# First softplus of a fused four-layer kernel: mask and polynomial moved from VectorE to GpSimd, the first drive and decay begun per half

## What is computed

```python
x = silu(conv(in_proj(ctx)) + conv_b)                 # u, 256 channels x 1024 tokens
dt_low, B, C = split(x_proj(x))
dt = softplus(dt_proj(dt_low) + dt_b)                 # delta
A = -exp(A_log)
for each token:                                       # for each of 16 states
    state = state * exp(dt * A) + (dt * u) * B        # decay, drive
    y = sum(state * C)
```

## Time and profile before

| | |
|---|---|
| Time of 3 runs, median (lowest to highest) | 925.41 us (924.95 to 927.92) |
| The profiled execution: time, span | 922.5 us, 920.6 us |
| Granted TensorE clock, mean | 0.927 |
| Busy: TensorE (matmul) | 831.2 us, 90% |
| Busy: VectorE | 646.9 us, 70% |
| Busy: ScalarE | 437.7 us, 48% |
| Busy: GpSimd | 439.3 us, 48% |
| Chain that ended last | TensorE 66%, VectorE 16%, GpSimd 6%, ScalarE 3% |

### The profile page before, as it was taken

One profiled execution on the slowest core, in us unless ns is written; L12 is line 12 of the kernel. 1 busy time (PEld: TensorE's weight loads), 2 busy tenths in 40 slices (PEclk: granted clock), 3 DMA queues, 4 the chain that ended last, 5 costly groups with the idle time before them and its releaser, 6 DMA issues.

```text
span 920.6 us, 12557 instructions
## 1 busy us (share of the span) xinstructions
PE 831.2 (90%) x4270; PEld 529.2 (57%) x4270; DVE 646.9 (70%) x1008; ACT 437.7 (48%) x825; POOL 439.3 (48%) x305
## 2 busy tenths in 40 slices
PE   7987888979999999998998979999996989989992
PEld 3322333336888888875776445555565865646661
DVE  4888999988999999987465556778758384322222
ACT  5752335332777777762555616655545412123330
POOL 3016666782588888862498002525501431613331
PEclk9986889797999999999999959999998997999996
DMA  6431222712122222212001113332135010261114
GB/s 234 168 141 69 71 76 81 326 58 96 47 92 93 92 92 92 92 46 69 18 1 35 56 37 87 97 108 74 53 104 197 1 69 0 87 201 47 47 46 159
DMA packets 28917, 81.86 MB, mean 89 GB/s; under 512 B 3424, under 2 KB 17648, under 8 KB 27472
## 3 DMA queue, kind: packets, MB, share of 16 engines
q1 hardware_dynamic: 26464, 73.38, 23.2%
q0 software_dynamic: 2256, 6.18, 1.9%
q10 hardware_dynamic: 144, 1.57, 0.4%
HBM read 65.77 MB, written 17.35 MB: 90 GB/s over the span
## 4 chain that ended last, share of the span: by engine, by line
PE 66%; DVE 16%; issue 6%; POOL 6%; ACT 3%; DMA 2%; SPq 0%; DVEq 0%; POOLq 0%; ACTq 0%
PE ps L853 12%; PE ps L875 6%; PE ps L1818 5%; PE ps L1442 5%; PE ps L565 4%; PE ps L1822 4%; PE ps L1860 3%; PE ps L995 3%; PE ps L556 3%; PE ps L1339 3%; POOL ZT L1078 2%; PE ps L1461 2%; PE ps L323 2%; PE ps L865 2%; DVE stats L300 2%
## 5 line engine op out<-in xcount | busy, mean ns | idle before, releaser
L853 PE MATMUL ps<-W,ZT 128*128 128x256 f32 x512 | 120.9, 379 | 0.0
L646 POOL TENSOR_TENSOR M<-M 128x1024 f32<-128x1024 f32 x32 | 75.3, 2354 | 85.8 <-DVE M L481 47.4
L1889 ACT ACTIVATE N<-ps 128x512 f32<-128x512 f32 x128 | 69.5, 595 | 77.8 <-PE ps L1822 77.8
L731 POOL TENSOR_TENSOR M<-N,M 128x1024 f32<-128x1024 f32 x32 | 76.3, 2385 | 52.8 <-DMA M<-dbl_scratch 27.2
L853 PEld LDWEIGHTS ps<-W,ZT 128*128 128x128 f32 x512 | 92.4, 190 | 10.0
L1818 PE MATMUL ps<-M,W 32*128 32x256 f32 x512 | 76.9, 434 | 10.9 <-DVE W L1916 5.7
L1910 DVE TENSOR_REDUCE W<-ps 128x4 f32<-128x1024 f32 x64 | 78.1, 1221 | 11.6 <-PE ps L1822 8.3
L701 DVE TENSOR_TENSOR_SCAN ps<-ps,M 128x512 f32<-128x512 f32 x64 | 78.7, 1230 | 6.1
L1822 PE MATMUL ps<-W,M 32*128 32x256 f32 x512 | 82.0, 415 | 0.0
L565 PE MATMUL ps<-M,ident 128*128 128x512 f32 x128 | 74.8, 738 | 7.4 <-DVE M L671 7.4
L662 DVE TENSOR_TENSOR_SCAN M<-ps,M 128x1024 f32<-128x1024 f32 x32 | 73.3, 2290 | 7.6 <-ACT ps L612 3.0
(11 more groups left out here) (305 smaller groups left out, 1738.2 us busy)
## 6 DMA issues: line engine op xcount, KB each, us to landing
M<-dbl_scratch SPq DMA_DIRECT2D x48, 512.0 KB, 3.7
W<-in_gu SPq DMA_DIRECT2D x1, 4800.0 KB, 18.0
W<-in_gu SPq DMA_DIRECT2D x1, 4352.0 KB, 14.1
slot_scratch<-in_slots SPq DMA_DIRECT2D x1, 3999.0 KB, 16.7
att_scratch<-W SPq DMA_DIRECT2D x28, 128.0 KB
M<-slot_scratch SPq DMA_DIRECT2D x3, 1032.0 KB, 9.7
W<-in_gu SPq DMA_DIRECT2D x2, 1536.0 KB, 7.6
W<-in_dn SPq DMA_DIRECT2D x1, 2176.0 KB, 18.9
```

Source lines behind the costliest of these rows:

```text
L646: nc.gpsimd.tensor_tensor(dBu[:, t, :], du[0][:, t, :], Bb[:, par, :], ALU.mult).then_inc(S("dBu_rdy"), 1)
L731: nc.gpsimd.tensor_tensor(dBu[:, t, :], du[1][:, t, :], Bb[:, par, :], ALU.mult).then_inc(S("dBu1_rdy"), 1)
L853: last = nc.tensor.matmul(ps[:, UBANK[j % 2], e * DIM:(e + 1) * DIM], ZT[:, c, t * P:(t + 1) * P], gu[:, c, 2 * j + e, :], start=(c == 0), ...
```

## The change

Mask and polynomial of the first softplus go from VectorE to GpSimd, as four instructions per half (the fused step of VectorE is two there). VectorE waits for them per half (`sp_poly`), and does A's sign and the clear of the PSUM columns between the halves. GpSimd's first drive waits for half 0 of `du` alone, but stands behind `softplus0_gpsimd` in GpSimd's stream. ScalarE begins the first decay of each half when that half's `du` is done, and evicts the second layer's step sizes behind each of the two decays instead of ahead of both; the store of the ternary weights is issued behind them.

```diff
-        def steps_to_sbuf(act, l, bank):
-            for t in range(2):
+        def steps_to_sbuf(act, l, bank, halves=(0, 1)):
+            for t in halves:
...
-        def softplus0_vector(dve, link):
-
-            small = lambda t: dA[:, t, :].bitcast(mybir.dt.uint32)
+        def softplus0_gpsimd(pool, link):
+
             for t in range(2):
                 e, q = dBu[:, t, :], hC[:, t, :]
-                dve.wait_ge(S("sp_exp"), 2 * t + 3)
-                link(nc.vector.tensor_scalar(dA[:, t, :], e, 2.0 ** -7, None, ALU.is_lt))
-                dve.wait_ge(S("sp_exp"), 2 * t + 4)
-                link(nc.vector.tensor_tensor(q, q, e, ALU.mult))
-                link(nc.vector.scalar_tensor_tensor(q, q, 1.0, e, ALU.add, ALU.mult))
+                pool.wait_ge(S("sp_exp"), 2 * t + 3)
+                link(nc.gpsimd.tensor_scalar(dA[:, t, :], e, 2.0 ** -7, None, ALU.is_lt))
+                pool.wait_ge(S("sp_exp"), 2 * t + 4)
+                link(nc.gpsimd.tensor_tensor(q, q, e, ALU.mult))
+                link(nc.gpsimd.tensor_scalar(q, q, 1.0, None, ALU.add))
+                nc.gpsimd.tensor_tensor(q, q, e, ALU.mult).then_inc(S("sp_poly"), 1)
+
+        def softplus0_vector(dve, link):
+
+            small = lambda t: dA[:, t, :].bitcast(mybir.dt.uint32)
             for t in range(2):
                 d, log = delta[0][:, t, :], hst[:, t, :]
                 dve.wait_ge(S("sp_ln"), t + 1)
+                dve.wait_ge(S("sp_poly"), t + 1)
                 link(nc.vector.copy_predicated(log, small(t), hC[:, t, :]))
                 link(nc.vector.scalar_tensor_tensor(d, d, 0.0, log, ALU.max, ALU.add))
                 nc.vector.tensor_tensor(du[0][:, t, :], d, u[0][:, t, :], ALU.mult).then_inc(S("du_done"), 1)
-            dve.wait_ge(S("a_done"), 1)
-            nc.vector.tensor_scalar(Aneg, Aneg, -1.0, None, ALU.mult).then_inc(S("delta_done"), 1)
-            dve.wait_ge(S("u_done"), 3)
-            nc.vector.memset(dAp.rearrange("p (b l) -> p b l", b=BATCH)[:, :, 0:1], 0.0).then_inc(S("delta_done"), 1)
+                if t == 0:
+                    dve.wait_ge(S("a_done"), 1)
+                    nc.vector.tensor_scalar(Aneg, Aneg, -1.0, None, ALU.mult).then_inc(S("delta_done"), 1)
+                    dve.wait_ge(S("u_done"), 3)
+                    nc.vector.memset(dAp.rearrange("p (b l) -> p b l", b=BATCH)[:, :, 0:1], 0.0).then_inc(S("delta_done"), 1)
             dve.wait_ge(S("delta_done"), 2)
...
-                act.wait_ge(S("sp_poly"), t + 1)
+                act.wait_ge(S("sp_poly"), 2 + t + 1)
...
-            steps_to_sbuf(act, 1, 0)
+            def decay(n, t):
+                if n or t:
+                    act.wait_ge(S("h_rdy"), n * 2 + t)
+                scale = Aneg[:, t, n:n + 1]
+                nc.scalar.activation(batches(dAp)[:, :, 1:], batches(delta[0][:, t, :])[:, :, 1:], ACT.Exp,
+                                     scale=scale).then_inc(S("dA_rdy"), 1)
+
+            act.wait_ge(S("delta_done"), 2)
+            for t in range(2):
+                act.wait_ge(S("du_done"), t + 1)
+                decay(0, t)
+                steps_to_sbuf(act, 1, 0, (t,))
             act.wait_ge(S("wq_done"), 1)
             act.dma_start(tern_dram, tq).then_inc(S("tern_out"), 16)
-            act.wait_ge(S("delta_done"), 2)
...
-            for n in range(NSTATE):
-                decays(n, n == 0)
+            for n in range(1, NSTATE):
+                for t in range(2):
+                    decay(n, t)
...
         def mamba0_gpsimd(pool):
-            pool.wait_ge(S("du_done"), 2)
-
             def steps(i, first):
                 for par in range(2):
                     pool.wait_ge(S(f"bc{par}"), 16 + i * 16)
                     for t in range(2):
+                        if first and par == 0:
+                            pool.wait_ge(S("du_done"), t + 1)
...
             taps_gpsimd(1)
+            softplus0_gpsimd(pool, link)
             mamba0_gpsimd(pool)
```

More of the change, by code:

```diff
@@ L464, in softplus0_scalar @@
                 nc.scalar.activation(hst[:, t, :], dBu[:, t, :], ACT.Ln, bias=1.0).then_inc(S("sp_ln"), 1)
+        def softplus0_gpsimd(pool, link):
+            for t in range(2):
+                e, q = dBu[:, t, :], hC[:, t, :]
+                pool.wait_ge(S("sp_exp"), 2 * t + 3)
[4 more added lines that the diff above has]
+                nc.gpsimd.tensor_tensor(q, q, e, ALU.mult).then_inc(S("sp_poly"), 1)
         def softplus0_vector(dve, link):
@@ L469, in softplus0_vector @@
             for t in range(2):
-                e, q = dBu[:, t, :], hC[:, t, :]
-                dve.wait_ge(S("sp_exp"), 2 * t + 3)
-                link(nc.vector.tensor_scalar(dA[:, t, :], e, 2.0 ** -7, None, ALU.is_lt))
-                dve.wait_ge(S("sp_exp"), 2 * t + 4)
-                link(nc.vector.tensor_tensor(q, q, e, ALU.mult))
-                link(nc.vector.scalar_tensor_tensor(q, q, 1.0, e, ALU.add, ALU.mult))
-            for t in range(2):
                 d, log = delta[0][:, t, :], hst[:, t, :]
                 dve.wait_ge(S("sp_ln"), t + 1)
+                dve.wait_ge(S("sp_poly"), t + 1)
                 link(nc.vector.copy_predicated(log, small(t), hC[:, t, :]))
@@ L601, in mamba0_scalar @@
             rows_to_sbuf(act, 1, 6)
-            steps_to_sbuf(act, 1, 0)
+            def decay(n, t):
[9 more added lines that the diff above has]
+                steps_to_sbuf(act, 1, 0, (t,))
             act.wait_ge(S("wq_done"), 1)
             act.dma_start(tern_dram, tq).then_inc(S("tern_out"), 16)
-            act.wait_ge(S("delta_done"), 2)
-            def decays(n, first):
+            for n in range(1, NSTATE):
                 for t in range(2):
[L609 to L613, removed]
-            for n in range(NSTATE):
-                decays(n, n == 0)
+                    decay(n, t)
                 if 10 <= n < 13:
```

## The result

The change makes the kernel slower: 935.92 us median of 4 runs (935.69 to 936.31) against 925.18 us (922.98 to 927.92) before, a ratio of 1.0101 with a 95% interval of 1.0078 to 1.0123. The forecast was 933.5 us, range 928.0 to 937.5, slower with a chance of 0.85. In a second series on another occasion the ratio was 1.0124 (1.0061 to 1.0188); there the absolute times of both kernels were lower (929.58 and 921.1 us). The ratios are those on record and not the quotients of these medians (which would be 1.0116 and 1.0092). In microseconds the first interval is 7.2 to 11.4, the second 5.6 to 17.3.

A forecast was written before the change was run, and what follows sets the result against it. The bound was the chain into the first scan loop, with VectorE ready last; GpSimd's serial polynomials and collisions delay the second scan from 70.99 to 79.1 us: 925.4 + 8.1 = 933.5 us, range 928.0 to 937.5.

The forecast's parts named there:

- Half 0: ready at 58.05: GpSimd's first-half polynomial, colliding with VectorE's ternary steps, is ready at 58.05 us instead of 54.0 undisturbed.
- The forecast's variant: GpSimd's add in half 0 not held by the packed ternary step: half ready at 55.2 us, total +5.3 us (930.7).
- GpSimd's one-input mask holds nobody: In the first softplus, GpSimd's mask (2.77 us) was taken to delay no VectorE instruction.
- Half 1: GpSimd's second-half polynomial: mask from 58.03, product waiting for VectorE until 62.0, add to 67.05, last product ending 69.5 us.
- The drive product is not early: GpSimd's first drive product, possible at 62.0 us by its data, queues behind the second half's polynomial until 69.5 us.
- The small edits at nothing: Moved decays, step-size evictions, column work and ternary store around the first scans cost nothing; the store at most 1 us.
- Pass through: From the second scan on, nothing absorbs the shift: the 8.1 us reach the kernel's end in full.
- My 2 us either side for the clock: TensorE clock stretches may fall elsewhere, 1.87 us per four row-spreading matmuls, either sign; 2 us allowed on each side.
- No conflict: Rival, no conflict with packed steps or none at all: 0.8 us later (926.2) or 3.0 us (928.4); chance 0.16.
- GpSimd locked out until the ternary work ends: Rival: ternary steps keep GpSimd out until 50.92 us, half 0 ready at 61.3, total +11.3 us (936.7); chance 0.08.
- The faster case: Rival: GpSimd's mask and add as cheap as its copy (0.95 us per 1024), second scan 6.0 us sooner, 919.4; chance 0.05.
- Every GpSimd instruction holding VectorE throughout: Rival: one-input GpSimd instructions also hold VectorE, first scan at 79.85 us, 12.3 us later (937.7); chance 0.06.

The follow-up runs named there:

- r2: The changed kernel with mask and polynomial left on VectorE, all its reordering kept; ratio 1.0009 to the kernel before.
- r3: The kernel before with only mask and polynomial moved to GpSimd, drives, decays and step sizes ordered as before; ratio 1.0115.
- r4: The kernel before with only the two masks moved to GpSimd, the polynomials staying on VectorE; ratio 0.9998.
- r5: The changed kernel without VectorE's last three ternary steps, leaving a later layer's quantised weights unfinished; 924.76 us in one execution.
- r6: The kernel before with masks as Relu and the linear step as a square on ScalarE, decays ahead of step sizes; ratio 0.9961.
- r7: As r6, with the very first drive product also moved from GpSimd to VectorE; ratio 0.9948 to the kernel before.

## Why the prediction was right, point by point

- **What bounds, and that the move replaces it.** Right. GpSimd's two polynomials in series are the new chain, to 70.45 us (forecast 69.5). r2 and r3 put the loss on the move: 1.0009 without it, 1.0115 with it alone.
- **Half 0: ready at 58.05.** Measured 58.63. How the ternary steps behave no row showed; that they collide like the 32-bit products was the right choice (third step to 53.57, forecast 52.98; add 5.77, forecast 5.8). The 0.6 us is the second ternary step, held by the mask for 0.7 us. The forecast's variant, in which the packed step does not hold the add, is refuted by the add's 5.77 us. (Its "4.9 us of blocked add and mask" doesn't follow from the list, which gives 3.16 + 0.69 = 3.85; the 55.2 us and 5.3 us of the variant do follow.)
- **"GpSimd's one-input mask holds nobody."** This step failed. It holds a two-input VectorE instruction for 0.7 to 0.8 us when it is first: steps of 4.07 us (r4, twice), the first copy 2.11 instead of 1.34. The rows I read (the copy at 190.34, the product at 197.46) began more than 1.1 us behind the start of the mask, or of the add's work, when it had let go. The rows were sound; the generalisation from them was not.
- **Half 1.** The product of 61.45 got in between VectorE's addition and its drive factor (62.11), where I had it wait for the latter. Its own end was the same (64.3 against 64.2), but it held the drive factor to 65.39, and that held the add: half 1 was ready 1.0 us later than forecast. This too comes from the mask's hold. By my times the addition ended at 60.7 us, so the product, asked for at 60.9, found the drive factor already running. Half 0 came 0.6 us late and the copy took 0.8 us longer, so that boundary came at 62.11, when the product (asked for at 61.45) was waiting; and a waiting product gets in at a boundary.
- **The drive product is not early.** Right: 70.40 us, behind half 1's polynomial, and the second copy behind it took 3.34 (forecast 3.5).
- **The small edits at nothing.** Right for decays and evictions. The ternary store took 7.2 us to landing instead of 5.1, and GpSimd stood idle for 2.17 us before the drive product at 86.74. The first 1.1 us of that it waited for the scan that used its buffer (83.39 + 2.29 = 85.68), as in every step; the row cost the other 1.0 us, which is the 1 us I had allowed. The scan that used the product waited 0.18 us, and that for its decay. The cover held, with some 1.4 us to spare.
- **Sum.** 8.1 us forecast, 8.9 measured at the second scan, 10.7 between the medians of the first series (9.3 by the ratio). The 0.8 us that the sum lacks goes back to the mask's hold, which I had put at nothing. "Pass through" holds against r4, but not against the profile of the kernel before: there the loop gave 3 us back (the clock stood at 0.50 until 85 us in both, which was 14 us of the loop before and 5 us of the changed one), and one profiled execution of the change lost 6 us near its end. The profiled spans are 13.4 us (first) and 5.2 us (repeat) longer than before, so the stage is what was predicted well; that the median of the first series came within 2.4 us of 933.5 is in part luck. My 2 us either side for the clock was too small for the loop's 3 us.
- **Rivals.** No conflict: refuted by the 5.41 and 5.77 us. GpSimd locked out until the ternary work ends: refuted, its product got in at 48.12, where the second ternary step ended. The faster case: mask and add took 2.78 us undisturbed (r5); the Trainium skill's "1-input is roughly line-rate" (GPSIMD Engine Reference, section 4.1 "Engine selection") doesn't hold for these two operations. Every GpSimd instruction holding VectorE throughout: refuted by r4, where each mask holds a step for 0.7 us and not for 2.8. The Trainium skill's exclusive lock for the whole instruction (SBUF — State Buffer, section "SBUF: two separate sides") agrees with the two-input products shown here, and with the one-input ones as far as they wait themselves (5.77 us), but not with how long those hold VectorE.

## What to carry to other kernels

Before moving a step to GpSimd, lay its instructions in time beside VectorE's two-input ones. In the rows shown here two-input instructions of the two engines never ran side by side: the second to come waited for the first (ternary step 5.41 us, product 3.61 us). Ask also which chain ends second (here TensorE's projections with ScalarE behind them, 0.4 us ahead of VectorE's), since the gain of a move is capped there, and what the receiving engine has queued behind the moved work. ScalarE took the masks and a part of the polynomial without lengthening any ternary step (3.36 us in r6 and r7).

## What the runs showed of the hardware that the rows before had not

- A one-input GpSimd instruction over 128x1024 f32 must wait for a running two-input VectorE instruction to its end (add 5.77 us instead of 2.78), but holds the next one only for 0.7 to 0.8 us (4.07 instead of 3.36; 2.11 instead of 1.34).
- The packed bf16 steps of VectorE, two inputs in SBUF, collide with GpSimd's products as the f32 ones do: step 5.41 us instead of 3.36, product 3.61 us instead of 2.35.
- Even VectorE's small one-input step over 128x32 (0.18 us before) took 1.01 us where GpSimd's add of half 1 began its work (65.39 us), in both profiles of the changed kernel.
